# Two buffers for the halves of h, ten more warming products, and the last two units' h turned by DMA

## The chip, the cores and the metric

The kernel runs on one core of one Trainium2 chip. The metric is the device time of one execution in microseconds (us). The engines are TensorE (matrix products; PE in the profile, its weight loads PEld), VectorE (DVE), ScalarE (ACT), GpSimd (POOL) and SyncE (SP, which only issues DMAs here). They run side by side and meet at semaphores.

## The reference, cut to what matters

```python
x = x + tanh(g_xattn[0]) * moe(layernorm(x), token_ids, ctx, ctx, ctx)
x = x + tanh(g_ffn[0]) * ffn(layernorm(x), gate_w, gate_b, val_w, val_b, out_w, out_b)

def moe(h, ids, Wg, Wu, Wd):          # expert of a token: ids // 6250, at most 3
    for e in range(4):                # all three weights of an expert are ctx[e], 512 x 512
        y = (silu(h @ Wg[e].T) * (h @ Wu[e].T)) @ Wd[e].T
        out = where(expert == e, y, out)

def ffn(x, ...):                      # D = 512, hidden = 2048
    return bit_linear(silu(bit_linear(x, gate)) * bit_linear(x, val), out)

def bit_linear(x, w, b):              # x rounded to 127 steps of its row's largest value,
    ...                               # w rounded to -1, 0, 1 times its mean absolute value
```

x is 4 x 512 x 512, so 2048 token rows of 512 float32. Gate and up weights of an expert are the same, so the kernel computes the product a once and forms gu = silu(a) * a.

## The kernel before, in words

**Stage 1, units.** The token rows are sorted by expert and padded to 19 units of 128 rows, each with one expert. TensorE first counts and places the tokens with small products; then GpSimd gathers each unit's rows (`gather`). For each unit j: VectorE takes mean and variance (`unit_stats`), GpSimd the reciprocal deviation (`unit_rstd`), VectorE writes the normalized h (`norm`, L1098). h has to be turned, so that its features lie on the partitions, and split into two float16 halves, high and low, since a float32 product is done as three float16 passes (high x high, high x low, low x high: `product`, L608, twelve products of 128x512 each). Product a, `silu`, `gu`; gu is turned on TensorE (`turn_gu`), split, and multiplied again (product y); `x1` adds it to the unit's rows, and GpSimd scatters the rows to memory with their mean and variance. A slot of TensorE (L646) is: turn gu of unit j-1, product a of unit j, turn h of unit j+1, product y of unit j-1.

**Two ways to turn h.** For units 0 to 8, 17 and 18, TensorE turns the float32 h with four identity products into PSUM (`turn_h`, L599), ScalarE writes the high half (`h_hi`, L849) and VectorE the low one (`h_low`, L1125). For the units in `H_DMA` (L41: 9 to 16), VectorE normalizes into the PSUM bank, ScalarE and VectorE split into one buffer `h16` (the memory of h_sb), and SP issues one DMA turn of both halves into one of two buffers `hT_dma` (`turn_h`, L268). The next unit's high half waits for that DMA (L855), since `h16` is one buffer. TensorE waits for it ahead of product a (L657).

**Between these**, ScalarE sums the absolute values of the FFN weights (`sum_abs`, L875), and after a small product for their mean GpSimd rounds (`round_pair`, L471) and ScalarE takes the sign (`sign_pair`, L887). How many of each stand in a slot is written in the tables SUMMED, ROUNDED and SIGNED (L37 to L39). SP's queue carries in order: weight loads, the turns of h, loads of the first eight tiles' scattered rows (`load_rows`), three bias loads, the turns of x.

**Front.** ScalarE and VectorE make the float16 halves of the expert weights; `keep_warm` (L592) runs WARM products on weights whose result nobody reads, up to the first h. `padding_before` (L1172) is small arithmetic that later gives the scatter's places; in VectorE's order it stands between the first `unit_stats` and the first `norm`. ScalarE's `w_copy(2)` waits for it.

**Stage 2, FFN.** 16 tiles of 128 rows. Per tile TensorE does gate and val in two halves c (16 products each, `gate`, `val`: eight a call) into a ring of three PSUM pairs, and `down` of the tile three before. VectorE empties the ring (`pre_gate`, L1220, `pre_val`, L1231), ScalarE takes silu, GpSimd multiplies (`z_pair`), VectorE takes the row maxima (`z_max`, `x_max`) that set the rounding scales, SP turns the rounded values by DMA. The order on each engine is written out by hand; VectorE's is the loop at L1320.

Of the kernel before, what the change touches and what calls it, by code (L numbers as in the profile page):

```python
# [5 lines left out]
def gated_block(nc, x, token_ids, ctx_w, g_xattn, g_ffn, gate_w, gate_b, val_w, val_b, out_w, out_b, out):  # L6
# [34 lines left out]
    H_DMA = range(9, 17)  # L41
    WARM = 20
# [12 lines left out]
    with ctx:  # L55
# [15 lines left out]
        h16 = h_sb[:, :].bitcast(f16)  # L71

        h_next = tern[:, 2 * G + 12:2 * G + 14, :].rearrange("p g d -> p (g d)").bitcast(f32)

# [145 lines left out]
        h_turned, hTlo_half = sem("h_turned"), sem("hTlo_half")  # L220
# [21 lines left out]
        o_last = sem("o_last")  # L242

# [7 lines left out]
        def _(sp):  # L251
# [16 lines left out]
            def turn_h(j):  # L268
                sp.wait_ge(hTlo_made, j + 1)
                if j >= H_DMA[0] + 2:  # L270
                    sp.wait_ge(a_done, j - 1)
                sp.dma_start_transpose(hT_dma[:, j % 2, :, :].rearrange("p i (k m) -> p (i k) m", m=P), h16).then_inc(h_turned, 16)
# [43 lines left out]

            for i, j in enumerate(H_DMA[:-2]):
                turn_h(j)
                if i in (0, 2):
                    load_weights(10 + i // 2)  # L320
# [5 lines left out]
            turn_h(H_DMA[-2])  # L326
            load_rows(2)
            load_rows(3)
            turn_h(H_DMA[-1])
            for t in range(4, EARLY):  # L330
                load_rows(t)
            sp.wait_ge(signed, bias_frees)
            sp.dma_start(bias_g, gate_b.partition_broadcast(P)).then_inc(bias_loaded, 16)
            sp.dma_start(bias_v, val_b.partition_broadcast(P)).then_inc(bias_loaded, 16)
            sp.dma_start(bias_o, out_b.partition_broadcast(P)).then_inc(bias_loaded, 16)
            turn_x(0)
# [20 lines left out]
        def _(pool):  # L357
# [22 lines left out]
            pool.wait_ge(consts_made, 3)  # L380
            nc.gpsimd.tensor_copy(ident16[:, :], ident32[:, :]).then_inc(consts16, 1)
# [105 lines left out]
            pool.wait_ge(consts32, 8)  # L487
# [85 lines left out]
        def _(pe):  # L573
# [72 lines left out]
            def slot(j, before=True, unit=True, after=True, gamma=None, between=None):  # L646
                first = isinstance(j, int) and j == 1
                if before and not first:
                    turn_gu(j - 1)
                if unit:  # L650
                    e4 = expert_of(j)
                    if first:

                        pe.wait_ge(wlo_made, 3)
                    low_made = (hTlo_made, j + 1)
                    if isinstance(j, int) and j in H_DMA:
                        low_made = (h_turned, 16 * (j - H_DMA[0] + 1))  # L657
                        pe.wait_ge(*low_made)
                    elif isinstance(j, int) and j == 0:
                        pe.wait_ge(hThi_half, 1)  # L660
                    else:
                        pe.wait_ge(hThi_made, j + 1)
                    product(a_of(j), *hT_of(j), e4, low_made,
                            j + 1 if isinstance(j, int) and j < E else None, between).then_inc(a_done, 1)
                if gamma is not None:
                    sum_gamma(gamma)
                if first:
                    turn_gu(j - 1)
                if after and not (isinstance(j, int) and j + 1 in H_DMA):
# [136 lines left out]
        def _(act):  # L806
# [42 lines left out]
            def h_hi(j):  # L849
                if j in H_DMA:  # L850
                    act.wait_ge(h_made, j + 1)
                    if j == H_DMA[0]:
                        act.wait_ge(hT_done, j)
                    else:
                        act.wait_ge(h_turned, 16 * (j - H_DMA[0]))  # L855
                    nc.scalar.activation(h16[:, 0:D], hT_ps[:, :], ACT.Copy, scale=H_SCALE).then_inc(hThi_made, 1)
                    return
# [39 lines left out]
            def slot(j):  # L897
# [13 lines left out]
                if 0 < j < UNITS - 1 and j + 1 not in H_DMA:  # L911
                    h_hi(j + 1)
                if j + 2 in H_DMA:
                    h_hi(j + 2)
# [7 lines left out]
                for p in sums[j > 1:]:  # L922
                    sum_abs(p)
# [114 lines left out]
        def _(dve):  # L1038
# [59 lines left out]
            def norm(j):  # L1098
                dve.wait_ge(rstd_made, j + 1)
                n = j % 2  # L1100
                if j in H_DMA:
                    dve.wait_ge(hTlo_made, j)
                elif j == H_DMA[-1] + 1:
                    dve.wait_ge(abs_summed, PAIRS)
                elif j == H_DMA[-1] + 2:
                    dve.wait_ge(h_turned, 16 * len(H_DMA))
# [18 lines left out]
            def h_low(j):  # L1125
# [7 lines left out]
                hi, lo = (h16[:, 0:D], h16[:, D:2 * D]) if j in H_DMA else hT_of(j)  # L1133
# [53 lines left out]

            w_low(0)
            w_low(1)
            unit_stats(0)  # L1190
            padding_before()
# [72 lines left out]
            for j in range(UNITS):  # L1264
# [7 lines left out]
                if early_norm:  # L1272
                    norm(j + 2)
                    unit_stats(j + 3)
# [45 lines left out]
            for t in range(TILES):  # L1320
# [7 lines left out]
                if 2 <= t < TILES - 2:  # L1328
# [3 lines left out]
                if 2 <= t < TILES - 2:  # L1332
# [4 lines left out]
                if 2 <= t < TILES - 2:  # L1337
                    x_scales(t + 2)
                if 1 <= t < TILES - 1:
                    z_max(t, 0)  # L1340
                pre_val(t, 1)
                if t == 0:
# [61 lines left out]
```

## Time and profile before

| | |
|---|---|
| median of 3 runs | 308.0 us (307.81 to 308.88) |
| profiled execution | 308.44 us |
| its span, first to last instruction | 306.7 us |
| mean granted TensorE clock | 0.991 |
| PE busy | 290.6 us, 95% of the span |
| DVE busy | 255.6 us, 83% |
| POOL busy | 234.6 us, 76% |
| ACT busy | 225.2 us, 73% |

The chain of work that ended last is by 79% TensorE, 7% VectorE and 6% DMA. The busy time of TensorE is modelled at its ends: a product of 512 columns is shown as 0.38 us long although the next one starts earlier, so distances between starts are safer than lengths. A row of a timeline merges neighbours of one line; the bracket at its end gives the engine's idle time ahead of it and what ended that. An idle engine that is not on the chain costs nothing.

### The profile page before, as it was taken

The page shows a single profiled execution, that of the slowest core. Times are in us where ns is not written, and L with a number is a line of the kernel's source. Part 1 is how long each engine was busy: PE and PEld are TensorE (multiplying, and loading weights), DVE is VectorE, ACT ScalarE, POOL GpSimd, SP SyncE. Part 2 cuts the span into 40 slices and gives each one's busy share as a digit, 9 for nine tenths or more (in the row PEclk, how much of TensorE's full clock was granted, in tenths as well). Part 3 has the DMA queues.
Part 4 walks back from the last instruction along what each step waited for, and adds up shares of the span by engine and source line. Part 5 has one row for each costly group of instructions (what it writes and reads, how often), then busy time and mean ns, then how long its engine had stood idle before and what let it go on. Part 6 is the DMA issues. An engine that isn't in the chain of part 4 may idle for free.

```text
span 306.7 us, 5303 instructions
## 1 busy us (share of the span) xinstructions
PE 290.6 (95%) x1422; PEld 141.3 (46%) x1437; DVE 255.6 (83%) x422; ACT 225.2 (73%) x311; POOL 234.6 (76%) x258
## 2 busy tenths in 40 slices
PE   1889999999999999999999999999999999999994
PEld 1445555544544545444334444444444444444453
DVE  5679977879979885799989899998898889887972
ACT  6949687767968756777997797777866886776650
POOL 3454863789888868957678799999889887977862
PEclk9979999999999999999999999999999999999998
DMA  7796787988886997213153635865444433543142
GB/s 251 245 316 208 293 292 275 385 249 260 229 189 138 246 261 315 88 60 87 37 100 71 118 74 120 126 150 98 110 114 109 88 73 79 120 86 87 52 103 106
DMA packets 58886, 49.10 MB, mean 160 GB/s; under 512 B 51119, under 2 KB 51119, under 8 KB 56560
## 3 DMA queue, kind: packets, MB, share of 16 engines
q1 hardware_dynamic: 54304, 35.43, 45.0%
q0 software_dynamic: 4560, 13.40, 12.8%
q8 instruction: 11, 0.18, 0.3%
q14 instruction: 11, 0.09, 0.1%
HBM read 28.35 MB, written 10.00 MB: 125 GB/s over the span
## 4 chain that ended last, share of the span: by engine, by line
PE 79%; DVE 7%; DMA 6%; issue 3%; ACT 2%; POOL 1%; DVEq 0%; ACTq 0%; POOLq 0%
PE banks L627 24%; PE banks L717 17%; PE banks L708 17%; PE banks L729 17%; DMA tern<-h_sb 5%; PE banks L634 2%; PE banks L602 1%; DMA xg<-in_x,gather_at 1%; PE banks L748 1%; DVE bn L1119 1%; POOL w_both L484 1%; DVE h_sb L1134 1%; DVE gu_sb L1138 1%; ACT turned L873 1%; DMA tok<-in_itok_BxS 1%
## 5 line engine op out<-in xcount | busy, mean ns | idle before, releaser
L627 PE MATMUL banks<-w_both,turned 128*128 x348 | 81.5, 383 | 1.4 <-ACT turned L873 0.8
L484 POOL TENSOR_TENSOR w_both<-raw 128x1024 f32<-128x1024 f32 (+1 forms) x32 | 75.0, 2343 | 6.7 <-DVE raw L1236 5.6
L953 ACT ACTIVATE w_both<-w_both,magic,raw 128x1024 f32 (+1 forms) x31 | 38.3, 1234 | 30.9 <-DVE raw L1253 30.9
L717 PE MATMUL banks<-tern,raw 128*128 128x512 bf16 x255 | 60.3, 379 | 0.7 <-DVE raw L1228 0.7
L708 PE MATMUL banks<-tern,raw 128*128 128x512 bf16 x251 | 59.9, 379 | 0.7 <-DVE raw L1236 0.4
L729 PE MATMUL banks<-tern,xg 128*128 128x512 bf16 x232 | 55.6, 379 | 0.5
L627 PEld LDWEIGHTS banks<-w_both,turned 128*128 128x128 f16 x348 | 34.3, 99 | 39.4 <-issue 5.3
L1228 DVE SCALAR_TENSOR_TENSOR raw<-banks,raw 128x1024 f32<-128x1024 f32 x32 | 41.0, 1280 | 8.0 <-issue 7.2
L1236 DVE SCALAR_TENSOR_TENSOR raw<-banks,raw 128x1024 f32<-128x1024 f32 x32 | 40.9, 1277 | 3.7 <-PE banks L717 3.7
L1243 DVE TENSOR_REDUCE raw<-w_both 128x1 f32<-128x1024 f32 (+1 forms) x32 | 38.8, 1211 | 4.0 <-POOL w_both L484 3.6
L717 PEld LDWEIGHTS banks<-tern,raw 128*128 (+1 forms) x256 | 24.9, 98 | 31.3 <-DVE raw L1228 1.6
L708 PEld LDWEIGHTS banks<-tern,raw 128*128 (+1 forms) x256 | 25.0, 98 | 30.8 <-DVE raw L1236 1.1
L978 ACT ACTIVATE raw<-raw 128x1024 f32<-128x1024 f32 x32 | 33.4, 1045 | 6.4 <-DVE raw L1228 6.4
L729 PEld LDWEIGHTS banks<-tern,xg 128*128 (+1 forms) x240 | 23.4, 98 | 28.4 <-issue 0.6
L530 POOL TENSOR_SCALAR w_both<-w_both,magic,one 128x1024 bf16<-128x1024 f32 x15 | 17.9, 1193 | 14.0 <-ACT w_both L953 13.3
L479 POOL TENSOR_SCALAR raw<-raw,inv_gam,magic 128x1024 f32<-128x1024 f32 x24 | 28.4, 1186 | 0.0
L387 POOL DMA_INDIRECT xg<-in_x,gather_at x19 | 20.3, 1070 | 9.8 <-DVE gather_at L1087 6.3
L890 ACT ACTIVATE tern<-raw,magic 128x1024 bf16<-128x1024 f32 x24 | 26.6, 1137 | 0.0
L884 ACT ACTIVATE tern<-raw 128x1024 bf16<-128x1024 f32 x24 | 25.3, 1053 | 0.3
L627 PE MATMUL banks<-w_both,tern 128*128 x108 | 24.9, 379 | 0.2
L545 POOL DMA_INDIRECT out<-raw x16 | 16.9, 1053 | 8.1 <-DVE raw L1261 3.6
L1138 DVE SCALAR_TENSOR_TENSOR gu_sb<-banks,gu_sb 128x512 f32<-128x512 f32 x19 | 12.8, 675 | 8.1 <-ACT gu_sb L869 8.0
(139 smaller groups left out, 412.5 us busy)
## 6 DMA issues: line engine op xcount, KB each, us to landing
raw<-in_ctx SPq DMA_DIRECT2D x4, 1024.0 KB, 6.8
raw<-in_L_ffn_gate_w SPq DMA_DIRECT2D x4, 1024.0 KB, 6.0
raw<-in_L_ffn_val_w SPq DMA_DIRECT2D x4, 1024.0 KB, 6.5
raw<-in_L_ffn_out_w SPq DMA_DIRECT2D x4, 1024.0 KB, 5.9
raw<-x_low SPq DMA_DIRECT2D x8, 257.5 KB, 3.8
raw<-x_high SPq DMA_DIRECT2D x8, 257.5 KB, 3.3
raw<-in_L_ffn_gate_b SPq DMA_DIRECT2D x1, 1024.0 KB, 8.2
raw<-in_L_ffn_val_b SPq DMA_DIRECT2D x1, 1024.0 KB, 9.6
```

The source lines that it names most:

```text
L479: nc.gpsimd.tensor_scalar(w, w, inv_gam[:, m:m + 1], magic[:, 0:1], ALU.mult, ALU.add).then_inc(rounded, 1)
L484: nc.gpsimd.tensor_tensor(z[:, t % 2, 2 * D * c:2 * D * c + width], g_sb[:, c, 0:width], v_sb[:, c, 0:width], ALU.mult).then_inc(z_made, 1)
L627: last = nc.tensor.matmul(acc[:, :], a[:, k * P:(k + 1) * P], flat(w[:, bass.ds(e4 + k, 1), :]), start=(k == 0 and i == 0), stop=(k == KD ...
L708: last = nc.tensor.matmul(ring[pair][:, b, :], flat(xiT[:, bass.ds(t % 2, 1), k, :]), tern[:, k * HC + 2 * c + b, :], start=(k == 0), stop ...
L717: last = nc.tensor.matmul(ring[pair][:, b, :], flat(xiT[:, bass.ds(t % 2, 1), k, :]), tern[:, G + k * HC + 2 * c + b, :], start=(k == 0), ...
L729: last = nc.tensor.matmul(to, flat(ziT[:, bass.ds(t % 2, 1), k, :]), tern[:, 2 * G + k, :], start=(k == 0), stop=(k == G - 1))
L890: nc.scalar.activation(flat(tern[:, bass.ds(2 * p, 2), :]), flat(raw[:, bass.ds(2 * p, 2), :]), ACT.Sign, bias=magic[:, 1:2]).then_inc(sig ...
L953: nc.scalar.activation(zq[:, a:b], flat(z[:, bass.ds(t % 2, 1), a:b]), ACT.Identity, scale=flat(sc[:, bass.ds(t, 1), 12:13]), bias=magic[: ...
L978: nc.scalar.activation(g_sb[:, c, :], g_sb[:, c, :], ACT.Silu).then_inc(s_made, 1)
L1228: v.scalar_tensor_tensor(g_sb[:, c, :], flat(ring[(4 * t + 2 * c + 1) % 3 if t else 0]), col(t, 3), bias_g[:, 2 * c * D:2 * (c + 1) * D], ...
L1236: v.scalar_tensor_tensor(v_sb[:, c, :], flat(ring[(4 * t + 2 * c + 2) % 3 if t else 1]), col(t, 4), bias_v[:, 2 * c * D:2 * (c + 1) * D], ...
L1243: v.tensor_reduce(col(t, 5 + c), z[:, t % 2, 2 * D * c:2 * D * (c + 1) + c], AX.X, ALU.max, apply_absolute_value=True).then_inc(zmax_made, 1)
```

## The change

Four parts.

- `H_DMA` becomes 9 to 18: h of units 17 and 18 is turned by DMA too. On SP's queue the turn of unit 17 stands between the row loads and the bias loads, that of unit 18 between the bias loads and the turns of x.
- `h16` becomes two buffers used in turn, the second in a part of the ternary weights that is written only by the last sign; the landing semaphore becomes two. The high half of unit j waits for the turn of unit j-2.
- `WARM` becomes 30, and VectorE does `padding_before` ahead of its first two low weight halves. One wait of GpSimd for the constants moves up.
- Orders: in slot 7 ScalarE's second sum stands ahead of the high half of unit 9; in the FFN, VectorE's `z_max(t, 0)` of tiles 1 and 2 goes behind `pre_val(t, 1)`, and the maximum and scales of x for tile 4 go to the end of slot 2.

```diff
-    H_DMA = range(9, 17)
-    WARM = 20
+    H_DMA = range(9, 19)
+    WARM = 30
-        h16 = h_sb[:, :].bitcast(f16)
+        h16 = tern[:, 2 * G + 14:2 * G + 16, :].rearrange("p g d -> p (g d)").bitcast(f16), h_sb[:, :].bitcast(f16)
+        def h16_of(j):
+            return h16[(j - H_DMA[0]) % 2]
+        def h_turn_of(j):
+            return h_turned[(j - H_DMA[0]) % 2], 16
+        def h_turned_to(j):
+            return h_turned[(j - H_DMA[0]) % 2], 16 * ((j - H_DMA[0]) // 2 + 1)
@@ SP
-                sp.dma_start_transpose(hT_dma[...], h16).then_inc(h_turned, 16)
+                sp.dma_start_transpose(hT_dma[...], h16_of(j)).then_inc(*h_turn_of(j))
-            for i, j in enumerate(H_DMA[:-2]):
+            for i, j in enumerate(H_DMA[:-4]):
                 turn_h(j)
@@
             load_rows(1)
-            turn_h(H_DMA[-2])
+            turn_h(H_DMA[-4])
             load_rows(2)
             load_rows(3)
-            turn_h(H_DMA[-1])
+            turn_h(H_DMA[-3])
             for t in range(4, EARLY):
                 load_rows(t)
+            turn_h(H_DMA[-2])
             sp.wait_ge(signed, bias_frees)
             sp.dma_start(bias_g, ...)
             sp.dma_start(bias_v, ...)
             sp.dma_start(bias_o, ...)
+            turn_h(H_DMA[-1])
             turn_x(0)
@@ POOL: pool.wait_ge(consts32, 8) moves from the first gather to the copy of ident16
@@ PE, ahead of product a
-                        low_made = (h_turned, 16 * (j - H_DMA[0] + 1))
+                        low_made = h_turned_to(j)
@@ ACT, h_hi(j)
-                    if j == H_DMA[0]:
-                        act.wait_ge(hT_done, j)
-                    else:
-                        act.wait_ge(h_turned, 16 * (j - H_DMA[0]))
+                    if j == H_DMA[0] + 1:
+                        act.wait_ge(hT_done, H_DMA[0])
+                    elif j > H_DMA[0] + 1:
+                        act.wait_ge(*h_turned_to(j - 2))
@@ ACT, slot(j)
+                late_sums = sums[j > 1:]
+                if j + 2 == H_DMA[0]:
+                    for p in late_sums:
+                        sum_abs(p)
+                    late_sums = ()
                 if j + 2 in H_DMA:
                     h_hi(j + 2)
@@ DVE, front
+            padding_before()
             w_low(0)
             w_low(1)
             unit_stats(0)
-            padding_before()
             norm(0)
@@ DVE, FFN loop
-                if 2 <= t < TILES - 2:
+                if 3 <= t < TILES - 2:
                     x_max(t + 2)                  # and so for x_gamma and x_scales
...
-                if 1 <= t < TILES - 1:
+                if 3 <= t < TILES - 1:
                     z_max(t, 0)
                 pre_val(t, 1)
+                if 1 <= t < 3:
+                    z_max(t, 0)
+                if t == 2:
+                    x_max(4)
+                    x_gamma(4)
+                    x_scales(4)
```

## Rows read from the trace of the kernel before

**Rows 1.** The page's first line.
```profile
span 306.7 us, 5303 instructions
```
**Rows 2.** Windows of TensorE: stretch, its sum, busy (instructions), granted clock, DMA share, GB/s.
```profile
18.00:18.50 0.50, 0.50 (x3) 0.70 0.91 377
...
21.50:22.00 0.50, 0.50 (x3) 0.89 0.93 393
```
**Rows 3.** Timeline of TensorE, front: start us, length us, line, operation [idle before <-releaser].
```profile
8.55 5.85 PE L594 MATMUL banks<-w_both 128*128 128x512 f16 x20
16.18 0.76 PE L681 MATMUL banks<-ident,h_sb 128*128 128x128 f32 x4 [1.78 <-DVE h_sb L1109]
...
17.59 3.03 PE L627 MATMUL banks<-w_both,turned 128*128 x8 [0.43 <-ACT turned L861]
20.42 1.06 PE L602 MATMUL banks<-ident,h_sb 128*128 128x128 f32 x4
...
22.31 2.83 PE L627 MATMUL banks<-w_both,tern 128*128 x12
```
**Rows 4.** Timeline of all engines, front: VectorE's low half of unit 1.
```profile
22.14 0.69 DVE L1134 SCALAR_TENSOR_TENSOR tern<-banks,tern 128x512 f16<-128x512 f32 x1 [1.43 <-ACT tern L865]
```
**Rows 5.** Timeline of TensorE, units 8 to 13: product y, once a slot.
```profile
68.88 2.76 PE L627 MATMUL banks<-w_both,turned 128*128 x12 [0.15 <-ACT turned L873]
...
75.05 2.75 PE L627 MATMUL banks<-w_both,turned 128*128 x12
...
80.80 2.75 PE L627 MATMUL banks<-w_both,turned 128*128 x12
...
86.42 2.75 PE L627 MATMUL banks<-w_both,turned 128*128 x12
...
92.52 2.76 PE L627 MATMUL banks<-w_both,turned 128*128 x12 [0.33 <-ACT turned L873]
...
98.69 2.75 PE L627 MATMUL banks<-w_both,turned 128*128 x12
```
**Rows 6.** Timeline of all engines, units 8 to 12.
```profile
65.59 0.60 ACT L856 ACTIVATE h_sb<-banks 128x512 f16<-128x512 f32 x1 [1.79 <-DVE banks L1112]
...
68.78 0.69 DVE L1143 SCALAR_TENSOR_TENSOR turned<-banks,turned 128x512 f16<-128x512 f32 x1 [0.45 <-ACT turned L873]
...
89.23 0.60 ACT L856 ACTIVATE h_sb<-banks 128x512 f16<-128x512 f32 x1 [2.02 <-DMA tern<-h_sb]
```
**Rows 7.** Source L272, the eight DMA turns of h: time from issue to landing.
```profile
DMA to landing us min/median/max: 3.1/4.1/5.8
```
**Rows 8.** The page's DMA issues, the last bias: KB, us to landing.
```profile
raw<-in_L_ffn_out_b SPq DMA_DIRECT2D x1, 256.0 KB, 10.1
```
**Rows 9.** Timeline of all engines, units 16 to 18.
```profile
112.01 0.43 SPq L335 DMA_DIRECT2D raw<-in_L_ffn_out_b  x1
...
115.67 0.60 PE L602 MATMUL banks<-ident,tern 128*128 128x128 f32 x4
...
116.11 2.75 PE L627 MATMUL banks<-w_both,turned 128*128 x12
...
117.11 0.68 DVE L1134 SCALAR_TENSOR_TENSOR turned<-banks,turned 128x512 f16<-128x512 f32 x1
...
125.41 5.62 PE L627 MATMUL banks<-w_both,turned 128*128 x24
...
129.70 2.56 DVE L1301 TENSOR_TENSOR out_gam<-gam,tanh_g 128x1 f32<-128x1 f32 x1
```
**Rows 10.** Timeline of all engines, tiles 1 to 3 of the FFN.
```profile
149.38 1.21 DVE L1243 TENSOR_REDUCE raw<-w_both 128x1 f32<-128x1024 f32 x1
...
151.84 1.90 PE L708 MATMUL banks<-tern,raw 128*128 128x512 bf16 x8 [0.42 <-DVE raw L1236]
...
155.72 0.68 DVE L1210 TENSOR_REDUCE raw<-banks 128x1 f32<-128x512 f32 x1
...
157.85 1.90 PE L717 MATMUL banks<-tern,raw 128*128 128x512 bf16 x8 [0.66 <-DVE raw L1228]
```

More of the change, by code:

```diff
@@ L219, in gated_block @@
         wlo_pool, w_scaled, w_copied = sem("wlo_pool"), sem("w_scaled"), sem("w_copied")
-        h_turned, hTlo_half = sem("h_turned"), sem("hTlo_half")
+        h_turned, hTlo_half = [sem(f"h_turned{n}") for n in range(2)], sem("hTlo_half")
         h_half, hT_half, hThi_half = sem("h_half"), sem("hT_half"), sem("hThi_half")
@@ L271, in turn_h @@
                     sp.wait_ge(a_done, j - 1)
-                sp.dma_start_transpose(hT_dma[:, j % 2, :, :].rearrange("p i (k m) -> p (i k) m", m=P), h16).then_inc(h_turned, 16)
+                sp.dma_start_transpose(hT_dma[:, j % 2, :, :].rearrange("p i (k m) -> p (i k) m", m=P), h16_of(j)).then_inc(*h_turn_of(j))
             def load_weights(n):
@@ L380, in _ @@
             pool.wait_ge(consts_made, 3)
+            pool.wait_ge(consts32, 8)
             nc.gpsimd.tensor_copy(ident16[:, :], ident32[:, :]).then_inc(consts16, 1)
@@ L485, in z_pair @@
                                         v_sb[:, c, 0:width], ALU.mult).then_inc(z_made, 1)
-            pool.wait_ge(consts32, 8)
             pool.wait_ge(gather_ready, 1)
@@ L851, in h_hi @@
                     act.wait_ge(h_made, j + 1)
-                    if j == H_DMA[0]:
-                        act.wait_ge(hT_done, j)
-                    else:
-                        act.wait_ge(h_turned, 16 * (j - H_DMA[0]))
-                    nc.scalar.activation(h16[:, 0:D], hT_ps[:, :], ACT.Copy, scale=H_SCALE).then_inc(hThi_made, 1)
+                    if j == H_DMA[0] + 1:
+                        act.wait_ge(hT_done, H_DMA[0])
+                    elif j > H_DMA[0] + 1:
+                        act.wait_ge(*h_turned_to(j - 2))
+                    nc.scalar.activation(h16_of(j)[:, 0:D], hT_ps[:, :], ACT.Copy, scale=H_SCALE).then_inc(hThi_made, 1)
                     return
@@ L921, in slot @@
                     w_scale(7)
-                for p in sums[j > 1:]:
+                for p in late_sums:
                     sum_abs(p)
@@ L1105, in norm @@
                 elif j == H_DMA[-1] + 2:
-                    dve.wait_ge(h_turned, 16 * len(H_DMA))
+                    for j_last in H_DMA[-2:]:
+                        dve.wait_ge(*h_turned_to(j_last))
                 if j == 0:
@@ L1132, in h_low @@
                 dve.wait_ge(hThi_made, j + 1)
-                hi, lo = (h16[:, 0:D], h16[:, D:2 * D]) if j in H_DMA else hT_of(j)
+                hi, lo = (h16_of(j)[:, 0:D], h16_of(j)[:, D:2 * D]) if j in H_DMA else hT_of(j)
                 v.scalar_tensor_tensor(lo, hT_ps[:, :], H_SCALE, hi, ALU.mult, ALU.subtract).then_inc(hTlo_made, 1)
@@ L1273, in _ @@
                     norm(j + 2)
-                    unit_stats(j + 3)
+                    if j + 3 < UNITS:
+                        unit_stats(j + 3)
                 gu(j)
@@ L1331, in _ @@
                     z_scales(t - 1)
-                if 2 <= t < TILES - 2:
+                if 3 <= t < TILES - 2:
                     x_gamma(t + 2)
@@ L1336, in _ @@
                     finish(0)
-                if 2 <= t < TILES - 2:
+                if 3 <= t < TILES - 2:
                     x_scales(t + 2)
-                if 1 <= t < TILES - 1:
+                if 3 <= t < TILES - 1:
                     z_max(t, 0)
                 pre_val(t, 1)
+                if 1 <= t < 3:
[4 more added lines that the diff above has]
+                    x_scales(4)
                 if t == 0:
```

## The prediction, made before the changed kernel ran

> **What bounds the kernel now.** I read the page first: which engine owns the chain that ended last. Then I followed that chain in order of time, because the shares of the page mix two stages. The reader is to see there long runs of TensorE broken in three places: a stretch of transfers and ScalarE work where the DMA turns of h begin, the same again four units later, and a stretch of VectorE and GpSimd in the first tiles of the FFN; TensorE's own rows at these places are [rows 5] and [rows 10]. Everywhere else only less TensorE work, or faster TensorE work, shortens the kernel. Last I read TensorE's own timeline with the granted clock beside it. The profiled execution took 308.44 us with a span of 306.7 [rows 1], so 1.74 us lie around the span; the median of the runs shown is 308.0, 0.44 lower. The sum below is made against 308.44. About 0.5%, 1.5 us, is what a measurement of this kernel can tell from no change.
>
> **Front: ten more warming products, and VectorE's reordering.** TensorE warms with 20 products from 8.55 on and is done at 14.4; then it stands 1.78 us until the first half of h exists [rows 3]. The granted clock falls from full to half within 18.0 to 18.5 and is back only within 21.5 to 22.0 [rows 2], that is, from 2.4 to 1.2 GHz, after this idle time. Its price: unit 0's first eight products take from 17.59 to the turn at 20.42, 2.83 us, and the next products of unit 0 and the turn fill the time to 22.31 [rows 3]. In an undisturbed slot 24 products and one turn take 5.62 us (80.80 to 86.42) [rows 5], and a turn takes 0.44 (115.67 to 116.11) [rows 9], so a product is 0.216. Twelve products and a turn at full clock are 3.03, so unit 1 would begin at 20.62 instead of 22.31: 1.69 us. But unit 1's last pass waits for the low half of a weight pair on VectorE, behind the low half of h, before which VectorE waited 1.43 us for ScalarE [rows 4]. That wait is all VectorE can win. The lesser counts: I take 1.4.
>
> The ten added products fill the idle 1.78 us. At 0.216 they end at about 16.4, some 0.2 past the 16.18 at which the first half of h was turned; moving the padding arithmetic off the path between statistics and normalization makes h ready a little earlier. Against that, VectorE's first two low halves of weights end later, under the wait for the gather. If all ten ran at half clock (0.43) they would end near 18.5 and cost about 2.3 instead of winning 1.4. Bounds of this part: 1.7 gained to 2.3 lost; I sit near the gain, because the last products before 14.4 already ran fast (20 in 5.85 us lies between 4.3 at 0.216 and 8.6 at 0.43, so some 7 were slow and 13 fast) [rows 3].
>
> The skill bears on this: the Trainium skill, TensorE: Matmul & The Clock Gate, section "What's actually happening", says that the number of slow matmuls at the start differs from run to run, because the activity monitor is not started by the kernel. The trace shows one such start only; by that rule the ten products could be partly slow, and the gain would differ by a few tenths to 2 us between runs.
>
> The moved wait for the constants on GpSimd stands behind memsets of the same engine, in time in which it only waits for the gather's list: nothing, at most 0.1 us if that cover were gone.
>
> **Units 9 to 16: two buffers for the halves.** In rows 5 a slot without a stall is 5.62 us. Two places are longer. At unit 8, TensorE waits 0.15 for ScalarE's high half of gu, and the slot from 68.88 to 75.05 is 6.17, 0.55 too long: 0.70 together [rows 5]. Before it ScalarE stood 1.79 us for VectorE's normalization of unit 9 with a sum of weights and a sign still to do behind it [rows 6]. The change puts the sum into that hole. The high half of gu comes earlier by the sum's length, VectorE's wait of 0.45 for it [rows 6] goes, and with it nearly the rest of this stall; what is late next is VectorE's product gu, which then ends just as TensorE asks for it. I take 0.5 of 0.70 (bounds 0.1 and 0.7).
>
> At units 11 and 12 the slots are 6.10 (86.42 to 92.52) and 6.17 (92.52 to 98.69) [rows 5]: 0.48 + 0.55 = 1.03 too long. The cause stands in ScalarE's row at 89.23: 2.02 us idle for the DMA turn of the unit before [rows 6], since both used the one buffer; the slowest turn took 5.8 us to land against a median of 4.1 [rows 7]. With two buffers the high half waits for the turn before last, landed a slot ago. Late next would be the turn itself: that one landed shortly before TensorE took it, and TensorE now comes earlier by what was won at unit 8. I take 0.9 (bounds 0.3 and 1.03).
>
> **Last two units.** Two turns leave TensorE: 2 x 0.44 = 0.88 [rows 9]. For each, VectorE normalizes into PSUM instead of SBUF and the high half no longer waits for TensorE; both lie in VectorE's and ScalarE's slack. On SP's queue the turn of unit 17 now stands before the three bias loads, and the turn of unit 18 behind them and before the first three turns of x. Behind unit 17's wait the biases are queued (VectorE asks for them in the last slot), behind unit 18's the turns of x, which the first FFN gate product waits for; both have some microseconds to spare. Unit 18's low half can be ready where VectorE's row at 117.11 ends, 117.8, and TensorE asks for it at 125.41 minus the 0.88 won and about 0.1, so 124.4 [rows 9]. Alone it lands in 3.1 to 5.8 us [rows 7], at 120.9 to 123.6: in time. But the last bias, issued at 112.01 [rows 9], took 10.1 us to land [rows 8], until 122.1, and now goes out about 2.5 us later. In between, the older row loads have drained, so I put its landing at about 123 and the turn at about 124.5: a stall of 0 to 6.0, taken as 0.3.
>
> **First FFN tiles.** The product gate(2,1) waits at 151.84 for VectorE's val evacuation, which stood behind a 1.21 us maximum at 149.38; val(3,0) waits at 157.85 for a gate evacuation behind the 0.68 us maximum of x at 155.72 [rows 10]. TensorE's waits are 0.42 + 0.66 = 1.08. The change moves both maxima behind the evacuations. Nothing is removed: the next gate evacuation comes later by the same work, and it is wanted only after a down product, 1.7 us later.
>
> These two parts don't add up. TensorE alone would win 0.88 - 0.3 + 1.08 = 1.66. VectorE, though, works without a gap from the bias scaling to that point, and its start is held by the 2.56 us of one tiny product at 129.70 [rows 9], which ended with GpSimd's rounding and does not come earlier when TensorE does. VectorE wins the moved 0.68, and by my estimate up to 0.6 more, because the row loads, and after them GpSimd, start earlier once the turns of h no longer wait for each other. So 0.7 to 1.3; I take 1.2, toward TensorE's 1.66.
>
> **Sum.** 1.4 + 0.5 + 0.9 + 1.2 = 4.0: 308.44 - 4.0 = 304.4 us. After 158 TensorE is busy without a gap to the tail, so what is won before is kept.
>
> **Rivals.** *Turn behind the biases (slower).* If unit 18's turn starts only when the last bias has landed (112.01 + 2.5 + 10.1 = 124.6) and then takes the worst 5.8, it lands at 130.4: a stall of 6.0 at unit 18's first product instead of 0.3, and 304.4 + 5.7 = 310.1. It decides against the gain above 127 (about 306.8, within the bound) and is slower than before above 130. For it: the 10.1 us of a transfer of 256 KB beside 5.8 at most for a turn [rows 7, 8]. Against it: these 10.1 us hold the older loads too, which then are gone. Beside this the Trainium skill, DMA: Bandwidth & Descriptors, section "Queues, rings and completion order", says that each DMA engine consumes one issuer's descriptors in order; by that the turn stands behind all of the bias.
>
> *Warming buys nothing.* The clock falls anyway, or the products end late: 304.4 + 1.4 = 305.8, with 0.3 of lateness 306.1. For it: the gap to unit 0's first product at 17.59 stays. Against it: the remaining gap is under 1 us instead of 1.78.
>
> *Late gains don't pass.* VectorE stays bound by GpSimd at the FFN's start and moves the wait elsewhere: the 1.2 shrinks to 0.2, 305.4. For it: VectorE's gapless stretch; against it: the order really is shorter by the two maxima.
>
> *VectorE slips past GpSimd.* It reaches the tiny product before GpSimd's last rounding begins, wins about 2.4, and TensorE's 1.66 and 0.6 more pass: 303.3.
>
> **How the numbers follow.** Forecast 0.58; warming buys nothing 0.12 (0.03 of it within the bound with other losses); late gains don't pass 0.12 (0.02 within); turn behind biases 0.14, half within, half slower; slip past 0.04. Faster: 0.58 + 0.09 + 0.10 + 0.04 = 0.81; same 0.03 + 0.02 + 0.07 = 0.12; slower 0.07. The range runs from 302.9, all parts at their better bounds (1.7 + 0.7 + 1.03 + 1.66, and 0.4 more of the slip), to 306.9, where the biases cost 2.5.
>
> **What would show it.** Right: a granted clock of 1.00 from 14 to 24 us; no ScalarE wait on the turn of h; slots of 5.6 us from unit 8 on; two groups of four turns fewer on TensorE; no wait of gate(2,1). Wrong: the clock at 0.50 after the longer warming; a gap ahead of unit 18's first product while the biases land; VectorE's tiny product still ending with GpSimd and a new TensorE wait in tiles 1 to 4.

## The result, and the profile after

The changed kernel took 307.07 us (median of 10 executions, 304.99 to 311.17), the kernel before, beside it, 308.69 (307.72 to 312.06): ratio 0.9942, 95% interval 0.9920 to 0.9963, a gain of 1.1 to 2.5 us. A second set of executions gave 306.73 against 308.37, ratio 0.9948 (0.9920 to 0.9976). One of the changed kernel's ten executions, the one of 311.17, was a slow one and is left out of the ratio. The sign was right, the size was not: 4.0 us were forecast, about 1.7 came, and 307.07 lies just above the range.

The profiled execution took 307.64 us with a span of 305.9 [rows 1]. The sum on record can be followed in it step by step. First the page's first line and TensorE's windows (columns as in rows 2): the clock of the front is mended, and it falls in a new place.

```profile
span 305.9 us, 5312 instructions
...
18.00:18.50 0.50, 0.50 (x4) 1.00 0.95 213
21.50:22.00 0.50, 0.50 (x5) 1.00 0.74 311
72.00:74.00 2.00, 1.45 (x5) 0.79 1.00 399
74.00:76.00 2.00, 2.00 (x6) 0.50 1.03 373
76.00:78.00 2.00, 2.00 (x10) 0.86 0.92 222
```

TensorE's timeline of the changed kernel, from the front to unit 18 (L638 is `product`, L645 `turn_gu`, L613 `turn_h`, L605 the warming):

```profile
8.55 8.18 PE L605 MATMUL banks<-w_both 128*128 128x512 f16 x30
16.57 0.60 PE L692 MATMUL banks<-ident,h_sb 128*128 128x128 f32 x4
...
17.52 1.90 PE L638 MATMUL banks<-w_both,turned 128*128 x8
19.25 0.60 PE L613 MATMUL banks<-ident,h_sb 128*128 128x128 f32 x4
...
20.69 2.83 PE L638 MATMUL banks<-w_both,tern 128*128 x12
...
64.29 0.60 PE L645 MATMUL banks<-ident,gu_sb 128*128 128x128 f32 x4
64.72 5.34 PE L638 MATMUL banks<-w_both,turned 128*128 x24
70.08 0.66 PE L645 MATMUL banks<-ident,gu_sb 128*128 128x128 f32 x4
72.55 4.45 PE L638 MATMUL banks<-w_both,tern 128*128 x12 [1.82 <-DMA tern<-tern]
76.83 2.75 PE L638 MATMUL banks<-w_both,turned 128*128 x12
...
82.59 2.75 PE L638 MATMUL banks<-w_both,turned 128*128 x12
...
88.20 2.75 PE L638 MATMUL banks<-w_both,turned 128*128 x12
...
93.82 2.75 PE L638 MATMUL banks<-w_both,turned 128*128 x12
...
99.44 2.75 PE L638 MATMUL banks<-w_both,turned 128*128 x12
...
125.58 2.75 PE L638 MATMUL banks<-w_both,tern 128*128 x12
...
156.89 1.90 PE L728 MATMUL banks<-tern,raw 128*128 128x512 bf16 x8 [0.34 <-DVE raw L1245]
```

Read against [rows 3], unit 1 begins at 20.69 instead of 22.31: the front's gain is there in this execution. At unit 8 the wait for ScalarE is gone and gu is turned at 70.08. Then product a of unit 9, the first unit with a DMA turn, waits 1.82 for that turn, and after it the twelve products take 4.45 us instead of 2.76, because the clock stands at 0.50. Product y of unit 8 begins at 76.83, in [rows 5] at 75.05: TensorE is 1.78 *later* where the forecast had it 1.9 (1.4 + 0.5) earlier. All that is missing in this execution is lost here, and a little more. From that product to the end of the span the changed kernel takes 305.9 - 76.83 = 229.07, the kernel before 306.7 - 75.05 = 231.65: it is better by 2.6 us, where 2.1 were forecast: units 11 and 12 have slots of 5.6 (88.20, 93.82, 99.44), unit 18 begins without a wait, and of the two waits of [rows 10] one of 0.34 is left.

The timeline of all engines answers to [rows 4], to the ScalarE row of [rows 6] and to VectorE's of [rows 9]: VectorE does not wait for unit 1's low half, ScalarE does not wait for a DMA turn, and VectorE's tiny product is as long as before.

```profile
20.52 0.69 DVE L1151 SCALAR_TENSOR_TENSOR tern<-banks,tern 128x512 f16<-128x512 f32 x1
...
88.90 0.59 ACT L867 ACTIVATE tern<-banks 128x512 f16<-128x512 f32 x1
...
129.87 2.56 DVE L1319 TENSOR_TENSOR out_gam<-gam,tanh_g 128x1 f32<-128x1 f32 x1
```

The ten turns of h by their source line, the last bias among the page's DMA issues, SP's issues, and the chain of waits (start, length, what):

```profile
DMA to landing us min/median/max: 3.0/5.4/6.7
```

```profile
raw<-in_L_ffn_out_b SPq DMA_DIRECT2D x1, 256.0 KB, 8.4
```

```profile
55.19 8.36 SPq L290 DMA_DIRECT2D raw<-in_L_ffn_out_w  x2
65.71 1.65 SPq L281 DMA_TRANSPOSE tern<-tern  x1
...
114.28 0.58 SPq L343 DMA_DIRECT2D raw<-in_L_ffn_gate_b  x1
114.90 0.44 SPq L344 DMA_DIRECT2D raw<-in_L_ffn_val_b  x1
115.39 0.43 SPq L345 DMA_DIRECT2D raw<-in_L_ffn_out_b  x1
118.57 1.34 SPq L281 DMA_TRANSPOSE tern<-h_sb  x1
```

```profile
65.03 0.67 DVE tern L1151
65.71 6.71 DMA tern<-tern
72.55 7.04 PE banks L638 x24
```

The turns are slower than in [rows 7] by their median, the bias faster than in [rows 8]. The second load in SP's first row (load 9, a quarter of out_w) went out at 63.23, 2.5 us ahead of the turn; before, 4.2 us lay between them (62.77 and 66.97). The turn landed after 6.71 us, the longest of the ten.

In all executions here the mean granted clock is either 0.994 and below or 0.997 and above. Of the changed kernel's 21 comparable executions (both sets) 7 are of the lower kind, with a median of 307.85; the other 14 have 306.18. The difference, 1.67, is close to the 4.45 - 2.76 = 1.69 of the row above; that it is the same loss in all seven is not shown. Of the kernel before, over five sets, 29 of 119 are of the lower kind, with a median of 309.51; the other 90 have 308.41. The profiled execution of the kernel before, with its clock of 0.991, was of the lower kind, and so is the changed kernel's (0.993): what the 14 others lose at unit 9, no trace shows. Between the two upper kinds, over several chips, the change wins 308.41 - 306.18 = 2.2 us.

### The profile page after: what moved, and what is told of

Read it like the earlier page. It is cut to its first block, busy times and chain, and to the rows that moved or that the text cites. A ratio compares the mean times of both kernels' runs of the same rounds, so it can differ in the third digit from the quotient of the medians.

```text
span 305.9 us, 5312 instructions
## 1 busy us (share of the span) xinstructions
PE 291.0 (95%) x1424; PEld 141.0 (46%) x1439; DVE 256.2 (84%) x422; ACT 225.1 (74%) x311; POOL 235.1 (77%) x258
## 4 chain that ended last, share of the span: by engine, by line
PE 77%; DMA 8%; DVE 6%; ACT 3%; issue 2%; POOL 2%; SPq 1%; DVEq 0%; POOLq 0%
PE banks L638 23%; PE banks L719 17%; PE banks L740 17%; PE banks L728 16%; DMA raw<-in_ctx 3%; DMA tern<-tern 2%; PE banks L645 2%; DMA raw<-x_low 2%; DMA xg<-in_x,gather_at 1%; PE banks L759 1%; DVE raw L1245 1%; DVE raw L1260 1%; SPq L300 1%; PE banks L613 1%; ACT tern L901 1%
## 5 line engine op out<-in xcount | busy, mean ns | idle before, releaser
L638 PE MATMUL banks<-w_both,turned 128*128 x324 | 74.4, 379 | 0.9 <-ACT turned L884 0.8
L638 PEld LDWEIGHTS banks<-w_both,turned 128*128 128x128 f16 x324 | 31.7, 98 | 36.0 <-issue 2.7
L638 PE MATMUL banks<-w_both,tern 128*128 x132 | 32.1, 394 | 1.8 <-DMA tern<-tern 1.8
L880 ACT ACTIVATE gu_sb<-banks 128x512 f32<-128x512 f32 x19 | 11.3, 596 | 18.9 <-PE banks L638 18.9
```

Source lines behind the costliest of these rows:

```text
L638: last = nc.tensor.matmul(acc[:, :], a[:, k * P:(k + 1) * P], flat(w[:, bass.ds(e4 + k, 1), :]), start=(k == 0 and i == 0), stop=(k == KD ...
```

## The experiments

Theory A: the front's 1.4 us was read from an execution of a rarer kind, and most executions have no such loss to win back. Theory B (the collision): the load of 1 MB that goes out close ahead of unit 9's turn delays that turn, and TensorE's wait for it eats what was won before. Rival to both: the other parts (two buffers, last units, FFN order) fell short.

**The change again, the front alone, the change without the front, and the loads moved.** Front: `WARM` and the place of `padding_before`, nothing else. Loads moved:

```diff
             load_weights(8)
-            gathers_landed(10)
-            load_weights(9)
...
                 turn_h(j)
-                if i in (0, 2):
-                    load_weights(10 + i // 2)
+                if i == 0:
+                    gathers_landed(10)
+                if i < 3:
+                    load_weights(9 + i)
```

Expected of the change again: 

> The changed kernel once more, for a second trace and a time on the same chip as the three others. First theory (collision): the DMA turn of unit 9 lands late because it is issued close behind a 1 MB weight load, and how close varies from execution to execution; so this trace shows unit 9's first product waiting between 0 and 2 us and the times spread from about 305 (no wait) to 307.9 (wait and half clock after it). Rival (slower turns): all turns land about 1.3 us later than before since the two buffers make them run beside other transfers; then the wait is there in every execution, near 1.8 us, and the spread has another cause.

Of the front alone on the kernel before: 

> The kernel before with only the thirty warming products and the padding arithmetic first. The front won 1.3 to 1.6 us in the changed trace. If that is kept: 1.3 us faster than before, 307.4 where before is 308.7. Collision: part of it is lost where the turns of h begin, since the gather of unit 10 and the last weight load there do not come earlier with the front; a wait of unit 9's first product of 0 to 2 us, so 307.4 to 309. Slower turns: one buffer is left, the turns land in 4.1 us median and nothing is lost: 307.4.

Of the change with 20 products and the old place of the padding: 

> The changed kernel with 20 warming products and the padding arithmetic in its old place. Collision: the turn of unit 9 has its old distance to the weight load and unit 9 does not wait, or less; the front's 1.3 us are lost, the 2 to 3.7 us of the wait are won back: about 306.0, faster than the changed kernel. Slower turns: the wait at unit 9 stays near 1.8 us, and the time is the changed kernel's plus 1.3, 308.4.

Of the change with the loads behind the turns: 

> The changed kernel with the weight load that stands before the turn of unit 9 put behind it, and the two later loads behind the turns of units 10 and 11. Collision: the turn of unit 9 lands in 3 to 5 us, its product does not wait, the clock stays up, and the time is 305.0 with little spread. Slower turns: landing stays above 5 us and the time at 307.0.

Measured against 308.37 before: the change again 306.73; the front alone 307.77, ratio 0.9982 (0.9960 to 1.0004); the change without the front 305.84, 0.9930 (0.9900 to 0.9959); the loads moved 305.47, 0.9897 (0.9864 to 0.9931). So the front is worth about 0.6 alone, and within the change it costs 0.9 (0.6 by the ratios), both inside the uncertainty: not 1.4. Moving the loads wins 1.3 more. The second trace of the change, here the timeline of all engines, shows the same place with another face. VectorE's statistics of unit 11 wait 1.55 for gathered rows, gu stands behind them, and TensorE waits for gu first and then for the turn:

```profile
70.03 0.69 DVE L1136 BATCH_NORM_STATS2 bn<-xg 128x6 f32<-128x512 f32 x1 [1.55 <-DMA xg<-in_x,gather_at]
...
71.58 0.66 PE L645 MATMUL banks<-ident,gu_sb 128*128 128x128 f32 x4 [1.47 <-DVE gu_sb L1155]
...
73.07 4.45 PE L638 MATMUL banks<-w_both,tern 128*128 x12 [0.84 <-DMA tern<-tern]
```

With the loads moved, from TensorE's timeline, unit 9 has no wait; a turn lands late elsewhere (unit 15's, behind two row loads):

```profile
70.35 0.64 PE L645 MATMUL banks<-ident,gu_sb 128*128 128x128 f32 x4
71.09 2.76 PE L638 MATMUL banks<-w_both,tern 128*128 x12
...
107.03 2.76 PE L638 MATMUL banks<-w_both,tern 128*128 x12 [1.29 <-DMA tern<-tern]
```

**Each part taken out, with the loads moved.** One edit each: the old front; `h16_of` always the second buffer, with the wait for the turn just before; `H_DMA` back to 9 to 16; the three order edits of the FFN undone.

Expected without the front: 

> The kernel with the loads behind the turns, but with 20 warming products and the padding arithmetic in its old place. Theory (the front's 1.4 us were read from an execution whose clock fell, which few do; other executions of before run at a mean clock of 1.0): the front is worth 0 to 0.6 us, so 305.5 to 306.1. Rival (the front is worth its 1.4 wherever nothing collides with it): 306.9.

With one buffer: 

> The kernel with the loads behind the turns, but with one buffer for the halves of h, each high half waiting for the turn before it. Theory (two buffers won the stall of units 11 and 12): 0.9 us slower than with two, 306.4, and waits of ScalarE for the turn of h in the trace. Rival (the two buffers win nothing, since the turns land later with them): 305.5.

Without the last two units: 

> The kernel with the loads behind the turns, but with units 17 and 18 turned on TensorE as before. Theory (the last two turns are worth 0.88 us of TensorE, of which VectorE and GpSimd at the FFN's start let 0.3 to 0.6 pass): 305.8 to 306.1. Rival (they cost, because the turns of units 17 and 18 stand among the row and bias loads): 305.0.

Without the FFN order: 

> The kernel with the loads behind the turns, but with VectorE's old order in the first FFN tiles. Theory (the order is worth what TensorE no longer waits for at gate(2,1) and val(3,0), 0.7 to 1.0): 306.2 to 306.5, with both waits back. Rival (the wait only moves): 305.5.

Measured, before at 308.44, as time and ratio: without the front 305.03, 0.9869 (0.9831 to 0.9907); one buffer 306.73, 0.9932 (0.9909 to 0.9956); without the last two units 306.17, 0.9909 (0.9874 to 0.9943); without the FFN order 306.37, 0.9937 (0.9904 to 0.9969). Against 305.47 that makes the buffers worth 1.3, the last units 0.7, the FFN order 0.9, the front minus 0.4. But 305.47 was measured on another chip; by the ratios, each against the kernel before on its own chip, they are 1.1, 0.4, 1.2 and minus 0.9. Each is uncertain by more than 1, so none of them is shown by its time alone. As they stand these parts reached their terms (0.9; 1.2 for the last two together), and nothing speaks for the rival. The traces show the waits come back in their old places: ScalarE's for the turn with one buffer,

```profile
81.10 0.60 ACT L867 ACTIVATE h_sb<-banks 128x512 f16<-128x512 f32 x1 [1.13 <-DMA tern<-h_sb]
88.30 0.60 ACT L867 ACTIVATE h_sb<-banks 128x512 f16<-128x512 f32 x1 [2.53 <-DMA tern<-h_sb]
```

and TensorE's 0.42 and 0.66 of [rows 10] without the FFN order:

```profile
148.82 1.90 PE L719 MATMUL banks<-tern,raw 128*128 128x512 bf16 x8 [0.42 <-DVE raw L1253]
...
154.84 1.90 PE L728 MATMUL banks<-tern,raw 128*128 128x512 bf16 x8 [0.66 <-DVE raw L1245]
```

The traces settle more than the times do. With VectorE's old FFN order TensorE waits 0.42 and 0.66 (once 0.65) at these two products in all six traces, with the new one only 0.34 at the second in all twelve: 0.74 won each time. From product y of unit 8 to that of unit 12, four slots, the kernels with one buffer take 23.39 to 25.16 us (six traces, median 23.78), those with two 22.60 to 22.63 in seven traces and 23.01 to 24.69 in five. So the buffers win about what was forecast, but not in every execution: in the two longest of the five (25 and 40 warming products, below) TensorE waits 1.59 and 1.47 for gu and then a turn, at unit 12 and unit 11.

Without the front TensorE's gap in front is still there, but the clock is 1.00 through it (all windows from 14 to 26). What is left of the change there is GpSimd's moved wait, which the forecast had put at nothing. GpSimd's timeline before, and without the front:

```profile
9.88 1.23 POOL L387 DMA_INDIRECT xg<-in_x,gather_at  x1 [6.26 <-DVE gather_at L1087]
```

```profile
9.24 1.23 POOL L399 DMA_INDIRECT xg<-in_x,gather_at  x1 [5.63 <-DVE gather_at L1103]
```

The first gather leaves 0.64 earlier: at 9.24 to 9.29 in all 13 traces with the wait moved, at 9.88 to 9.93 in all five without, though VectorE writes the gather's list at about 8.8 in both. The first turn of h, on TensorE, begins at 15.80 instead of 16.18 [rows 3], with a shorter gap:

```profile
8.54 5.88 PE L605 MATMUL banks<-w_both 128*128 128x512 f16 x20
15.80 0.76 PE L692 MATMUL banks<-ident,h_sb 128*128 128x128 f32 x4 [1.39 <-DVE h_sb L1126]
...
17.21 1.90 PE L638 MATMUL banks<-w_both,turned 128*128 x8 [0.43 <-ACT turned L872]
```

Unit 0 begins at 17.21 here, at 17.52 in the change with its 30 products.

What the ten products are worth by themselves can be read from unit 1's first product in all the traces. On the kernel before with 20 products it begins at 22.31 and 22.43 where the clock fell in front (the profiled execution; the loads moved, below), but at 20.76 and 20.80 in two traces where it did not (the early sum alone and the held load, both below). With 30 products and the old wait of GpSimd it begins at 20.80. With GpSimd's wait moved it begins at 20.38 to 20.57 with 20 products (four traces) and at 20.45 to 21.59 with 30 (seven). So the front wins 1.5 us where the clock would have fallen, and without that fall the ten products win nothing and can cost up to a microsecond. TensorE's timeline and windows of the held load's trace, the front of before without a fall:

```profile
8.58 7.21 PE L595 MATMUL banks<-w_both 128*128 128x512 f16 x20
16.23 0.76 PE L682 MATMUL banks<-ident,h_sb 128*128 128x128 f32 x4 [0.43 <-DVE h_sb L1110]
...
20.80 2.85 PE L628 MATMUL banks<-w_both,tern 128*128 x12
...
18.00:20.00 2.00, 2.00 (x13) 1.00 0.82 289
```

**Is the collision the change's own? The loads moved on the kernel before; the early sum and unit 15's turn on the best one.** The early sum is ScalarE's second sum of slot 7, which the change puts ahead of unit 9's high half.

Expected of the kernel before with the loads moved: 

> The kernel before with one edit alone: load 9 goes behind the DMA turn of unit 9, loads 10 and 11 behind those of units 10 and 11. Theory (collision made by the change): in the kernel before the turn of unit 9 lands in 4.1 us and TensorE waits little for it, so moving the load alone wins 0 to 0.4 us: about 308.1, ratio 0.998 to 1.001. Rival (the order of the loads is worth as much by itself): the 1.3 to 1.6 us that it won on the changed kernel, about 306.9, ratio 0.995.

Of the change, loads moved, old front, the sum of slot 7 late again: 

> The changed kernel with the loads behind the turns and the front of before (the fastest so far, 305.03), and now ScalarE's second sum of slot 7 back in its old place behind the high half of unit 9. Theory (the early sum is worth the 0.5 of the forecast): about 305.5, TensorE again waits at unit 8 for ScalarE's high half of gu. Rival (its gain goes to VectorE's product gu, which is late next): 305.0 to 305.1, and TensorE waits for gu_sb or for the turn of h instead.

Of the same with the early sum, and `turn_h(H_DMA[-4])` moved ahead of `load_rows(0)`: 

> The changed kernel with the loads behind the turns and the front of before, and the DMA turn of unit 15 put ahead of the first two row loads on SP's queue. Theory (a turn waits for the bytes that stand ahead of it on its queue): the turn of unit 15 lands in about 4 us instead of up to 7.3, the wait ahead of its first product (0 to 1.3 us) goes, 304.5 to 305.0. Rival (the row loads are what comes late): they wait for the turn's halves, start some 2 us later, GpSimd and VectorE come late at the start of the FFN and the time rises to 305.5 to 306.5.

Measured, before at 309.39 on this chip: 308.52, ratio 0.9955 (0.9925 to 0.9985); 305.62, 0.9869 (0.9823 to 0.9915); 306.98, 0.9920 (0.9891 to 0.9950). The first came nearest to the rival: the order of the loads is worth about as much on the kernel before, though the interval just reaches the 0.998 of the theory. The second trace has the 0.15 of [rows 5] back at unit 8, but its ratio is that of the kernel with the early sum: 0.5 us of TensorE's time there can't be told in the total. The third, meant as an improvement, is worse by about 1.5 (by the ratios), at the upper end of what the rival expected. The later row loads aren't shown to be the reason: its trace has three new small waits ahead of the FFN (0.28, 0.20, 0.35), all for turns of h, none for rows.

**How many warming products; and the collision made certain.** `WARM` 25 and 40 with the loads moved; and in the kernel before load 9 is held:

```diff
             gathers_landed(10)
+            sp.wait_ge(hThi_made, H_DMA[0] + 1)
             load_weights(9)
```

Expected of 25: 

> The changed kernel with the loads behind the turns, and 25 warming products instead of 30. Theory (the warming runs past h): with 30 the first turn of h began at 16.3 to 17.5 although its first half was there at about 15.6; five products of 0.216 fewer let it begin at about 15.7, unit 0's products begin at 17.0 to 17.3, and the time falls by 0.3 to 0.9 against the 30 products (305.5), to 304.6 to 305.2. Rival (the overrun is hidden, since unit 0 waits for ScalarE's half anyway): unit 0 begins where it did, 305.5 plus or minus 0.2.

Of 40: 

> The same with 40 warming products. Theory (the warming runs past h): ten more products of 0.216 end 2.2 us later, at 18.5 to 19.6; the first turn of h and all behind it come 2.2 later, 307.3 to 308.0, with full clock in the front. Rival (idle time and other waits of the front swallow it): 305.5 to 306.3.

Of the load held until unit 9's high half: 

> The kernel before, with SP holding load 9 (1 MB) until the high half of unit 9's h is written, so that it stands close ahead of that unit's DMA turn in every execution. Theory (the turn waits for the load's bytes, and the clock falls in the wait): the turn of unit 9 lands in 6.5 to 8.5 us instead of 4.1, TensorE waits 2 to 4 us ahead of unit 9's first product, the granted clock falls to 0.5 for some 2 us and costs 1.7 more: 311.5 to 314 us. Rival A (the wait comes without the fall of the clock): 310 to 312. Rival B (the turn does not wait for the load, the landing of 6.7 in the changed kernel came from elsewhere): 308 to 309.

Measured, before at 308.65: 306.12, 0.9928 (0.9898 to 0.9958); 308.67, 1.0011 (0.9987 to 1.0035); 308.81, 1.0000 (0.9971 to 1.0028). Forty products cost 2.6 us against 25; the first turn of h begins at 19.58. Twenty-five did not win what was expected over 30. Behind 30 products the turn of h began at 16.33 to 17.48 (30 of them took 7.95 to 9.09 us), but TensorE could begin it from about 15.8: filling the gap costs up to what it saves. Twenty products took 5.72 to 7.22 us in eight traces, and the clock fell behind the two shortest of them (5.72 and 5.85), which left the longest gaps (1.89 and 1.78). This is how the clause on record from the Trainium skill (TensorE: Matmul & The Clock Gate, "What's actually happening"), that the number of slow products differs from run to run, shows here.

The held load did what theory B says to the wait, from the chain and from TensorE's timeline:

```profile
65.48 7.45 DMA tern<-h_sb
```

```profile
73.07 2.76 PE L628 MATMUL banks<-w_both,tern 128*128 x12 [2.20 <-DMA tern<-h_sb]
```

The turn took 7.45 instead of 4.1 and TensorE waited 2.20, but in this execution the clock stayed at 1.00, and the total is that of before: the wait came as the theory had it, the time as rival B had it. Four of the 12 executions have the lower clock, not many more than without the held load. Units 11 and 12 then hardly stalled any more (slots of 5.83 and 5.61): a wait put in at one transfer went with a shorter one at another. The price expected, 3 to 5 us, was wrong.

**Which edit brings the collision?** The early sum, taken out of the change and put alone into the kernel before.

Expected of the change without it: 

> The changed kernel with ScalarE's second sum of slot 7 back behind the high half of unit 9. Theory (the early sum brings TensorE to unit 9 before its turn has landed): the stretch from the turn of gu of unit 7 to product y of unit 8 is 9.5 us, with no wait for the turn of h, no execution with the granted clock at 0.994 or below, and the time falls to 305.8 to 306.3 from the changed kernel's 306.9. Rival (the loads come late against TensorE for another reason, the earlier gathers or the front): 12 to 13 us there, the low clock in a third of the executions as before, 306.9 to 307.5.

Of the kernel before with it: 

> The kernel before with the early sum alone. Theory (the early sum is what brings the collision): the stretch at unit 9 is 10.3 to 13 us instead of 9.5, and the 0.5 us that it wins there alone are lost again: 308.4 to 310. Rival (the early sum is harmless by itself): 9.0 us there, and the time 0.5 less, 307.8 to 308.1.

Measured, before at 308.64: 306.36, 0.9942 (0.9907 to 0.9978), the ratio of the change with it (0.9942, 0.9948), and 308.57, 0.9999 (0.9965 to 1.0033). So in the total the early sum shows in neither. Worked out from the traces, from the turn of gu of unit 7, gu(7), to product y of unit 8 (65.54 to 75.05 before):

| load 9 | early sum | us, one trace each |
|---|---|---|
| ahead of unit 9's turn, 2.5 to 2.8 before gu(7) is turned | no | 9.51 (before), 9.50 (front alone) |
| ahead, 0.7 to 1.6 before | yes | 12.54, 13.03 (the change), 10.32 (no front), 10.43 (early sum alone) |
| ahead, 1.6 before | no | 10.46 (change without early sum) |
| ahead, 0.7 after gu(7) | no | 12.25 (held load) |
| behind the turn | no | 9.51 (before), 9.50 (best kernel, late sum) |
| behind the turn | yes | 8.95 to 9.01 (eight traces) |

Neither theory nor rival holds as written: the stretch is long with and without the early sum wherever load 9 goes out late against TensorE, and the early sum is worth 9.50 - 8.97 = 0.53 once the load is out of the way. The change's two traces, both of the lower kind of clock, lose 3.0 and 3.5 us in this stretch against the kernel before; the three others with the load 1.4 to 1.6 before gu(7), of the upper kind, lose 0.8 to 1.0, which is the nearest to what the change's 14 other executions lose. The clock goes with the load too: of the executions of the changed kernel and its two variants with load 9 ahead, 14 of 44 have the lower clock, of its nine variants with the loads behind, 3 of 80. Why load 9 goes out late is seen, not tested: SP holds it for the landing of unit 10's gather, issued at 55.27 in the change's trace, 8.0 us ahead of the load; in the kernel before at 56.52, 6.3 us ahead of it.

## Why the prediction was right or wrong

**Front, forecast 1.4: the step that failed first.** As a reading of two traces it held: 20.69 against 22.31. As a term for the median it did not: the sum took a loss of one execution for a loss of all. The loss of [rows 2, 3] is a fall of the clock that fewer than a quarter of the executions of the kernel before have, if all 29 of 119 with the lower clock have it there; of the four traces with that front the clock fell in the two of the lower kind and stayed in the other two, and there unit 1 began at 20.76 and 20.80, about where the change's two traces have it (20.69, 20.99). The front alone won 0.6; within the change it cost 0.9, and with the loads moved 0.4. GpSimd's wait, put at nothing, already brings h 0.4 earlier, and in the four traces that have it without the longer warming the clock did not fall in front. The rival *Warming buys nothing* (305.8) is nearest for this part, but for another reason: the clock mostly did not fall, with or without it.

**Unit 8, forecast 0.5: won in the stretch (0.53), not in the total.** The forecast named VectorE's product gu as late next and left the transfers out of this step. Of the five traces with load 9 at most 1.6 us ahead of gu(7), gu was late in four, because VectorE stood behind unit 11's gathered rows, and the DMA turn of unit 9 in the two of the changed kernel as it is. The sum held no term for either, although all steps ahead of unit 9 brought TensorE nearer to them. In the profiled execution 1.9 us of gain and 1.8 more went here; moving the loads gives back 1.3 in the median. In the kernel before the same move wins about as much, so this collision explains the changed profile. The shortfall in the median is, by the measured parts, the front and the early sum: 4.0 - 1.4 - 0.5 = 2.1, against 1.6 to 1.8 measured.

The Trainium skill (DMA: Bandwidth & Descriptors, "Queues, rings and completion order") has each DMA engine take turns, packet by packet, between the queues that have work for it. No trace shows the packets, but the landings go with it: in the five traces with load 9 at most 1.6 us ahead of gu(7), GpSimd's gather of unit 11 took 6.2 to 7.7 us to land, in the ten with the loads moved 3.6 to 5.4.

**Two buffers, forecast 0.9: right in size.** In the change there is no wait of ScalarE for a turn and the slots are 5.6; the four slots are shorter by 1.2 in the median of the traces, and the time is by 1.1 to 1.3, with its uncertainty. The stall is not gone in every execution: what came late next was gu and the turn itself, as the forecast feared of the turn.

**Last two units and FFN order, forecast 1.2: right, at the better end** (0.7 and 0.9 by the times, 0.4 and 1.2 by the ratios, each uncertain by more than 1). VectorE's tiny product begins and ends as in [rows 9], held by GpSimd, yet of TensorE's 1.08 of waits in [rows 10] only 0.34 is left. *Late gains don't pass* is refuted in its mechanism, though 305.4 is nearer to the result than the forecast. *Turn behind the biases* did not happen: unit 18's turn, 3.2 us behind the last bias, landed in 6.1, the bias in 8.4, and unit 18 began without a wait; in other kernels it waited 0.2. *VectorE slips past GpSimd* did not happen.

The best version of all is the change with the loads behind the turns and the old front: 305.03, 1.3% faster than before.

What stays open: why the order of the loads is worth 0.5 to 2.3 us on the kernel before, whose own trace shows no wait at unit 9 and whose trace with the loads moved is no shorter. Executions that collide there, not traced, could explain it; against that speaks the held load, which brought the wait in its trace and left the time as it was. Open too is why the clock fell behind the wait at unit 9 in the change's two traces and not behind the longer one there.

## What to carry to other kernels

A term read from one execution is worth its share of executions: before pricing a fall of the clock, compare that execution's mean clock with those of the others. When steps bring an engine earlier to a transfer, price the transfer: what it waits for on its queue, and which large load goes out just ahead. An idle gap is filled with the work that fits it; beyond that, warming is work.

## What the hardware showed unexpectedly

The clock does not fall after every gap of a length. It fell to 0.50 after 1.82 us ahead of unit 9 in the change, and stayed at 1.00 after 2.20 in the kernel with the held load; it fell in the front behind a gap of 1.78 [rows 2, 3] and stayed behind one of 1.39. The DMA turn of one unit, always the same 256 KB, took 3.0 to 8.4 us over all the traces; unit 9's took 6.7, 7.2 and 7.45 close behind a load of 1 MB (the change twice, the held load) and 4.1 in the kernel before.
